# Mixer gate of a two-layer recurrent/attention kernel: from units of two channel tiles by two chunks to units of one tile by four

## The reference, cut to what matters

```python
proj = einsum('bld,pd->blp', x, W_in)              # x: 2048 x 256
gate = proj[..., :INTER]                           # INTER = 4096 channels, 8 groups of 512
hbc  = silu(conv(proj[..., INTER:INTER+CONV_DIM])) # x, B, C of the state space part
...
g  = y * silu(gate)                                # y: the state space output
gg = g * rsqrt(mean(g * g, per group) + EPS)       # norm over the 512 channels of a group
return einsum('bli,di->bld', gg * norm_weight, W_out)
```

## Time and profile before

| | |
|---|---|
| three runs | 2546.90, 2548.81, 2554.18 us; median 2548.81 |
| the profiled execution, its own time | 2549.98 us |
| its span, first to last instruction | 2548.0 us |
| PE busy in the span | 2262.3 us (89%) |
| DVE, ACT, POOL busy | 1850.7, 1433.1, 1266.7 us |
| mixer, from its first load to its last product | 219 to 1518 us of the span |
| slots 0 and 126 start at | 255.37 and 1486.49 us |

### The profile page before, as it was taken

How to read it: one execution, slowest core, us unless ns; L and a number is a source line. 1 busy time by engine, 2 the same in 40 slices (tenths; PEclk the granted TensorE clock), 3 DMA queues, 4 the chain that set the end, 5 groups by cost and what they waited for, 6 DMA issues and landing times. The chain is left out here.

```text
span 2548.0 us, 45522 instructions
## 1 busy us (share of the span) xinstructions
PE 2262.3 (89%) x16164; PEld 1795.5 (70%) x16164; DVE 1850.7 (73%) x3268; ACT 1433.1 (56%) x2447; POOL 1266.7 (50%) x1243
## 2 busy tenths in 40 slices
PE   4995999999999999999999962699999996699993
PEld 3785788888888888888888852588888885344332
DVE  5875777877777777777777746677777776777755
ACT  1333887878787778788778841122222224266661
POOL 3451676777767687676876640344545450000000
PEclk9998999999999999999999985799999998799996
DMA  2003112112121121211111120100000002222214
GB/s 89 1 22 110 49 48 81 45 48 86 53 73 53 44 82 52 82 45 65 61 61 45 53 75 17 35 21 28 21 27 28 21 14 83 70 75 77 80 61 136
DMA packets 91518, 141.17 MB, mean 55 GB/s; under 512 B 23328, under 2 KB 60544, under 8 KB 90048
## 3 DMA queue, kind: packets, MB, share of 16 engines
q1 hardware_dynamic: 89280, 133.96, 15.8%
q10 hardware_dynamic: 2048, 4.72, 0.6%
HBM read 118.12 MB, written 20.32 MB: 54 GB/s over the span
## 5 line engine op out<-in xcount | busy, mean ns | idle before, releaser
L1057 DVE SCALAR_TENSOR_TENSOR mix_cv<-mix_pp,mix_cw,mix_cv 128x384 f32<-128x384 f32 (+4 forms) x864 | 490.7, 571 | 215.2 <-ACT mix_cv L979 194.3
L1004 ACT ACTIVATE mix_lm<-mix_pd 128x512 f32<-128x512 f32 x256 | 153.3, 599 | 207.9 <-PE mix_pd L895 205.9
L1196 POOL TENSOR_TENSOR ffn_hl<-ffn_h,ffn_hh 128x512 fp32r<-128x512 f32 x112 | 144.9, 1294 | 249.9 <-ACT ffn_hh L1254 249.9
L839 POOL TENSOR_TENSOR mix_ce<-mix_ce,mix_cv 128x1024 f32<-128x1024 f32 x112 | 266.7, 2381 | 0.0
L75 PE MATMUL mix_pp<-l0in_XH,mix_w_lo 128*128 128x384 f32 (+2 forms) x576 | 242.9, 422 | 22.6 <-DVE mix_w_lo L1045 16.3
L961 PE MATMUL mix_px<-mix_wo,mix_z 128*128 128x256 f32 x1024 | 257.4, 395 | 0.0
L1719 DVE TENSOR_REDUCE att_tops<-att_psc 128x1 f32<-128x512 f32 (+3 forms) x384 | 189.9, 550 | 56.2 <-PE att_psc L1667 32.2
L845 POOL TENSOR_TENSOR mix_zt<-mix_zsq 128x256 f32<-128x256 f32 x128 | 94.2, 736 | 266.4 <-ACT mix_zsq L1012 266.4
L1743 ACT ACTIVATE att_pr<-att_pst 128x1024 f32<-128x1024 f32 (+7 forms) x256 | 156.5, 657 | 104.0 <-PE att_pst L1684 73.6
L1254 ACT ACTIVATE ffn_hh<-ffn_h 128x512 fp32r<-128x512 f32 x112 | 71.1, 635 | 249.0 <-DVE ffn_h L1277 249.0
L961 PEld LDWEIGHTS mix_px<-mix_wo,mix_z 128*128 128x128 f32 x1024 | 187.4, 193 | 20.8
(11 more groups left out here) (331 smaller groups left out, 6881.0 us busy)
## 6 DMA issues: line engine op xcount, KB each, us to landing
mix_ce<-ecs SPq DMA_DIRECT2D x112, 512.0 KB, 3.7
mix_w_raw<-in_w_in SPq DMA_DIRECT2D x8, 1280.0 KB, 5.5
a_part<-att_sums SPq DMA_DIRECT2D x32, 256.0 KB, 5.1
ffn_raw<-in_wgu SPq DMA_DIRECT2D x56, 128.0 KB, 2.2
mix_ll<-cs SPq DMA_DIRECT2D x384, 4.0 KB
mix_wo<-in_w_out SPq DMA_DIRECT2D x8, 512.0 KB, 6.4
ffn_draw<-in_wd SPq DMA_DIRECT2D x28, 128.0 KB, 2.1
q<-qkv_part SPq DMA_DIRECT2D x24, 128.0 KB, 1.9
```

What stands on the lines that cost most here:

```text
L839: pool.tensor_tensor(ce[o][:, :, :], ce[o][:, :, :], cv[:, CT_C, cols_of(c)].unsqueeze(1).to_broadcast([P, GH, Q]), ALU.mult).then_inc(ce_ ...
L1004: act.activation(lm[o][:, 4 * i:4 * i + 4, :].rearrange("p h l -> p (h l)"), pd[:, :], ACT.Exp).then_inc(l_done, 1)
L1057: last = dve.scalar_tensor_tensor(out, of, cw[:, g, ct, 3 - d:4 - d], out, ALU.mult, ALU.add)
```

## The change

A gate unit now holds one channel tile by four chunks (512 columns) instead of two channel tiles by two chunks (256 columns each): six matmuls of 512 columns in place of twelve of 256. Four units serve four chunks, so a unit has to be ready earlier: slot `c` makes unit c+3 (`LEAD = 3`) instead of c+1, and `sg` grows to two buffers of four chunks.

`w_raw` shrinks to the 768 columns per half of the `x`, `B`, `C` channels. The gate's part comes first, into the same buffer, at SP's step `c % 16 == 1` (512 KB); `wo` follows at step 2; the other 768 KB come at step 6, after POOL has split the gate's part (`wg_split`). The pieces are split in another order, in slots 2 to 5 (gate), 7 to 10 (the rest) and 11 (`wo`). For the first group the gate's raw weights pass through the second half of `sg`, and ACT no longer waits for `wo`.

```diff
-        w_raw = s.sb("w_raw", [P, KD, NXBC + GX])
+        w_raw = s.sb("w_raw", [P, KD, NXBC])
...
-        sg = s.sb("sg", [P, 2, NX, 2 * Q])
+        sg = s.sb("sg", [P, 2, NX, 4 * Q])
...
+        SPLIT_AT = (2, 3, 4, 5, 7, 8, 9, 10, 11)
+        LEAD = 3
...
-                load_weights(0)
+                sp.dma_start(w_raw[:, :, :], w_in[0][:, :, 0:NXBC]).then_inc(wx_in, 16)
+                sp.dma_start(sg[:, 1, 0:KD, :], w_in[0][:, :, NXBC:]).then_inc(wg_in, 16)
+                sp.dma_start(wo[:, 0, :, :], w_out[0]).then_inc(wo_in, 16)
...
+                    if c % 16 == 1 and g < G0 - 1:
+                        wait(sp, gate_done, 16 * g)
+                        sp.wait_ge(wx_split, 2 * (g + 1))
+                        sp.dma_start(w_raw[:, :, 0:GX], w_in[g + 1][:, :, NXBC:]).then_inc(wg_in, 16)
                     if c % 16 == 2 and g < G0 - 1:
+                        wait(sp, op_done, 16 * g)
+                        sp.dma_start(wo[:, (g + 1) % 2, :, :], w_out[g + 1]).then_inc(wo_in, 16)
+                    if c % 16 == 6 and g < G0 - 1:
                         wait(sp, proj_done, 36 * g)
-                        wait(sp, gate_done, 16 * g)
-                        wait(sp, op_done, 16 * g)
-                        sp.wait_ge(wx_split, 2 * (g + 1))
-                        sp.wait_ge(wg_split, 2 * (g + 1))
-                        load_weights(g + 1)
+                        sp.wait_ge(wg_split, 2 * (g + 2))
+                        sp.dma_start(w_raw[:, :, :], w_in[g + 1][:, :, 0:NXBC]).then_inc(wx_in, 16)
...
-                    if live and 4 <= c % 16 < 13 and c // 16 < G0 - 1:
-                        split(c // 16 + 1, c % 16 - 4)
+                    if live and c % 16 in SPLIT_AT and c // 16 < G0 - 1:
+                        split(c // 16 + 1, SPLIT_AT.index(c % 16))
...
                     wait(pe, w_done, u)
-                    wait(pe, ss_done, u - 2)
-                    for t in range(2):
-                        chans = slice(NXBC + (u % 2 * 2 + t) * P, NXBC + (u % 2 * 2 + t + 1) * P)
-                        for i in range(KD):
-                            last = matmul3(pe, pgt[:, t * 2 * Q:(t + 1) * 2 * Q], w_hi[:, o, i, chans], w_lo[:, o, i, chans],
-                                           XH[:, i, at], XL[:, i, at], i == 0, i == KD - 1)
+                    wait(pe, ss_done, u - LEAD - 1)
+                    for i in range(KD):
+                        last = matmul3(pe, pgt[:, :], w_hi[:, o, i, chans], w_lo[:, o, i, chans],
+                                       XH[:, i, at], XL[:, i, at], i == 0, i == KD - 1)
...
-                    if 0 <= c + 1 < NC:
-                        gate(c + 1)
+                    if 0 <= c + LEAD < NC:
+                        gate(c + LEAD)
...
-                act.wait_ge(w_in_s, 32)
+                act.wait_ge(wx_in, 16)
+                act.wait_ge(wg_in, 16)
...
-                        wait(act, z_done, u // 2 * 2 - 2)
-                        act.activation(sg[:, u // 2 % 2, u % 2 * 2:u % 2 * 2 + 2, :].rearrange("p k l -> p (k l)"),
-                                       pgt[:, :], ACT.Silu).then_inc(w_done, 1)
+                        wait(act, z_done, u // 4 * 4 - 4)
+                        if u == 4:
+                            act.wait_ge(wg_split, 2)
+                        act.activation(sg[:, u // 4 % 2, u % 4, :], pgt[:, :], ACT.Silu).then_inc(w_done, 1)
...
-                        dve.wait_ge(w_done, p // 2 * 2 + 2)
+                        dve.wait_ge(w_done, p // 4 * 4 + 4)
```

More of the change, by code:

```diff
@@ L691, in mixer @@
         tabs_in, norm_in, const, made, self_v, zeroed = (s.sem(n) for n in ("tabs_in", "norm_in", "const", "made", "self_v", "zeroed"))
-        w_in_s, wx_split, wg_split, wo_split, hi_made, hi_first = (
-            s.sem(n) for n in ("w_in", "wx_split", "wg_split", "wo_split", "hi_made", "hi_first"))
+        wx_in, wg_in, wo_in, wx_split, wg_split, wo_split, hi_made, hi_first = (
+            s.sem(n) for n in ("wx_in", "wg_in", "wo_in", "wx_split", "wg_split", "wo_split", "hi_made", "hi_first"))
         cs_in, ecs_in = ([s.sem(f"{n}{j}") for j in range(2)] for n in ("cs_in", "ecs_in"))
@@ L764, in _ @@
             def _(sp):
-                def load_weights(g):
-                    sp.dma_start(w_raw[:, :, :], w_in[g]).then_inc(w_in_s, 16)
-                    sp.dma_start(wo[:, g % 2, :, :], w_out[g]).then_inc(w_in_s, 16)
-                load_weights(0)
+                sp.dma_start(w_raw[:, :, :], w_in[0][:, :, 0:NXBC]).then_inc(wx_in, 16)
+                sp.dma_start(sg[:, 1, 0:KD, :], w_in[0][:, :, NXBC:]).then_inc(wg_in, 16)
+                sp.dma_start(wo[:, 0, :, :], w_out[0]).then_inc(wo_in, 16)
                 sp.dma_start(cw[:, :, :, :], conv_w).then_inc(tabs_in, 16)
@@ L809, in split @@
                 def split(g, piece):
-                    o = g % 2
+                    o, k = g % 2, piece // 2 % 2
                     if piece < 8:
[L813 to L817, removed]
+                        part, done, loaded = (slice(NXBC, NXBC + GX), wg_split, wg_in) if piece < 4 else (slice(0, NXBC), wx_split, wx_in)
+                        cols = part.stop - part.start
+                        raw, hi, lo = w_raw[:, k, 0:cols], w_hi[:, o, k, part], w_lo[:, o, k, part]
+                        if piece % 4 == 0:
+                            pool.wait_ge(loaded, 16 * g + 16)
                         if piece % 2 == 0:
@@ L823, in split @@
                     else:
+                        pool.wait_ge(wo_in, 16 * g + 16)
                         pool.tensor_tensor(wo[:, o, :, :], wo[:, o, :, :],
@@ L826, in split @@
                                            ALU.mult).then_inc(wo_split, 1)
-                pool.wait_ge(w_in_s, 32)
                 split(0, 8)
@@ L875, in gate @@
                 def gate(u):
-                    o, at = u // 16 % 2, slice(u // CPS % 2 * (T // 2) + u % CPS // 2 * 2 * Q, u // CPS % 2 * (T // 2) + (u % CPS // 2 + 1) * 2 * Q)
+                    o, at, chans = u // 16 % 2, slice(u % 16 // 4 * 4 * Q, (u % 16 // 4 + 1) * 4 * Q), slice(NXBC + u % 4 * P, NXBC + (u % 4 + 1) * P)
                     if u % 16 == 0:
@@ L952, in _ @@
                         pe.wait_ge(zs_done, p + 1)
-                        pe.wait_ge(w_done, min(c + 2, NC))
+                        pe.wait_ge(w_done, min(c + LEAD + 1, NC))
                         pe.matmul(pgt[:, 0:1], zs[:, :], one[:, :], start=True, stop=True).then_inc(n_done, 1)
@@ L984, in squash @@
                     act.activation(conv_tile(k), conv_tile(k), ACT.Silu).then_inc(conv_done, 1)
-                act.wait_ge(w_in_s, 32)
+                act.wait_ge(wx_in, 16)
+                act.wait_ge(wg_in, 16)
                 for part in (slice(0, NXBC), slice(NXBC, NXBC + GX)):
-                    act.activation(w_hi[:, 0, :, part], w_raw[:, :, part], ACT.Copy).then_inc(hi_first, 1)
+                    raw = w_raw[:, :, :] if part.start == 0 else sg[:, 1, 0:KD, :]
+                    act.activation(w_hi[:, 0, :, part], raw, ACT.Copy).then_inc(hi_first, 1)
                 act.wait_ge(const, 48)
@@ L1020, in _ @@
                         act.activation(btok[o][:, :], pmisc[:, 0:N0], ACT.Copy).then_inc(btok_ready, 1)
-                    if 0 <= c + 1 < NC:
-                        u = c + 1
+                    if 0 <= c + LEAD < NC:
+                        u = c + LEAD
                         act.wait_ge(gate_done, u + 1)
-                        wait(act, z_done, u // 2 * 2 - 2)
-                        act.activation(sg[:, u // 2 % 2, u % 2 * 2:u % 2 * 2 + 2, :].rearrange("p k l -> p (k l)"),
-                                       pgt[:, :], ACT.Silu).then_inc(w_done, 1)
+                        wait(act, z_done, u // 4 * 4 - 4)
+                        if u == 4:
+                            act.wait_ge(wg_split, 2)
+                        act.activation(sg[:, u // 4 % 2, u % 4, :], pgt[:, :], ACT.Silu).then_inc(w_done, 1)
                     if c < 0:
@@ L1044, in _ @@
                     dve.wait_ge(hi_first, 1 if part.start == 0 else 2)
-                    dve.tensor_tensor(w_lo[:, 0, :, part], w_raw[:, :, part], w_hi[:, 0, :, part].bitcast(F32),
+                    dve.tensor_tensor(w_lo[:, 0, :, part], w_raw[:, :, :] if part.start == 0 else sg[:, 1, 0:KD, :], w_hi[:, 0, :, part].bitcast(F32),
                                       ALU.subtract).then_inc(done, 2)
@@ L1078, in _ @@
                         dve.tensor_tensor(z[p % 2][:, :, :], py[:, :].rearrange("p (k l) -> p k l", k=NX),
-                                          sg[:, p // 2 % 2, :, p % 2 * Q:(p % 2 + 1) * Q], ALU.mult).then_inc(z_done, 1)
+                                          sg[:, p // 4 % 2, :, p % 4 * Q:(p % 4 + 1) * Q], ALU.mult).then_inc(z_done, 1)
                     if ks:
```

## The result

The changed kernel takes 2558.72 us, the median of six runs (2557.53 to 2561.23); the kernel before took 2548.86 beside it. The ratio is 1.0036, with a 95% interval of 1.0026 to 1.0047. So it is slower by about 0.3%, where 2546.0 was forecast, and it lies above the forecast's range of 2540 to 2556.

A forecast was written before the change was run, and what follows sets the result against it. PE was taken to wait for ACT's chain from the decays to zs, or to be level with it. The terms -1.0 + 1.7 - 0.7 - 1.3 + 1.2 - 2.7 = -2.8 us took 2548.81 to 2546.0 us, range 2540 to 2556.

The forecast's parts named there:

- second load: SP's 768 KB load at step 6 delays the tables queued behind it; PE stalls 0.25 us seven times, +1.7 us.
- The 4.2: Forecast landing time in us of the 768 KB load after its issue: 5.5 - 1.3.
- The lower bound: For the second load's stall: the shortest landing seen, 5.2 us, was said to make it 0.
- the second load holds up the tables: Rival at step 6's load: a stall of 1.7 us per group makes the kernel 0.3% slower; chance 0.10.
- gate unit, 128 times: PE's cheaper gate matmuls save 0.03 us in a quarter of the 128 slots, -1.0 us; bounds 0 and -7.7.
- wait at step 2: With the large load gone from step 2, PE's one wait for the tables there goes, -0.7 us.
- start: ACT's first copy waits for the two parts of w_in, not for wo; -1.3 us, bounds 0 and -1.3.
- warm-up: Two more gate units between fills in slots -3 and -2 cost at most 2.5 us; half taken, +1.2 us.
- tail: Slots 125 and 126: L954 waits for zs, no longer the gate's Silu; 1.36 us each, -2.7 us.
- The bound of 0: For the tail's gain: PE, with less work there, falls to the lower clock and gives it back.
- PE is the bound after all: Rival in the mixer's slots: the gate units' whole 7.7 us counts, -9.5 us in all, 2539.3 us; chance 0.10.
- The ends give nothing: Rival: warm-up costs its full 2.5 us, the tail gives back its gain; +1.2 us, 2550.0 us; chance 0.12.

The follow-up runs named there:

- e6: Changed kernel with 384 KB of step 6's load left ahead of the tables and the rest moved behind ce; 2551.49 us, ratio 1.0005.
- e7: Changed kernel with wo's 512 KB load moved from step 2 to step 6, so 1280 KB stand ahead of the tables; 2575.27 us, ratio 1.0095.
- e5: Changed kernel with the old gate units, one chunk ahead, and the old sg, so the split loads alone; 2555.60 us, ratio 1.0029.
- e4: Kernel before with the new gate units alone (512 columns, LEAD = 3, larger sg), loads as before; 2548.31 us, ratio 0.9992.
- e8: The changed kernel as it is, measured again in a second series against the kernel before; 2556.41 us, ratio 1.0031.
- e9: Changed kernel with one matmul in place of the three of each gate product, low parts left out; 2568.38 us, ratio 1.0072.
- e1: Changed kernel with the 768 KB load and its two waits moved behind the tables and ce of step 6; 2547.78 us, ratio 0.9998.
- e12: Changed kernel with ScalarE issuing one partition of the 768 KB load in slot 5, SP the other 127 at the end of step 6; 2727.61 us.

## Why the prediction was wrong

The step that failed is the size of the second load's stall: "Give the small tables 0.2 us after the load: PE stalls about 0.25 us, seven times, +1.7 us". It measured 1.10 to 1.49 us, seven times, +8.8. In slot 53 the 1.49 come apart like this: the load went out 5.57 us into the slot (5.47 forecast), it took 4.70 us and not 4.2, and the last table came 0.85 us behind it and not 0.2. The 4.2 took 1.3 us off the landing of 1280 KB for 512 KB less. The 1.3 is what 512 KB add behind a load that is already running, and e6 and e7 agree with it (some 2.5 to 3.0 us per 1024 KB). But between loads that go out by themselves the landing fell by less, from 5.5 us for 1280 KB to 4.7 for 768 KB; why, no run shows. The 0.2 had no row at all.

The lower bound was misread as well. The 5.2 us that "makes it 0" does so only when the same 1.3 us are taken off; as it stands it gives 1.24 us in each group, +8.7 us, which is what came. Still the 8.8 lie inside the bounds, 0 to +23 us, and the rival "the second load holds up the tables" named the right cause, though its own condition, 1.7 us in each group, was not reached. Its chance of 0.10 was too small for a term whose two parts no row showed. Put 8.8 in place of 1.7, and the sum is +4.3 us, about 2553. So the load accounts for 7.1 of the 12.7 us between the forecast and the first result; that the time left the range is also the work of the rest, which follows.

The mechanism was told rightly: the load goes out where POOL's split ends, and `rl` and `ll` queue behind it. That they wait there for its transfer was my estimate, with no row; the trace of the changed kernel shows it, with no small packet in the 3.80 us behind the load's issue and the last table 0.85 us behind its landing.

The other terms, forecast and measured:

| term | forecast | measured |
|---|---|---|
| gate unit, 128 times | -1.0 | 0: the slots keep their length within 0.03 us; PE's wait for `zs` grew by some 0.06 us where there was one |
| second load | +1.7 | +8.8 |
| wait at step 2 | -0.7 | -0.5, slot 81 |
| start | -1.3 | -1.2 (e5, load to slot 0) |
| warm-up | +1.2 | +1.3 (e4), +1.8 beside the split load |
| tail | -2.7 | -3.65 in the first profile, -5.9 in e8; -2.6 with both at the full clock |

The tail was forecast by the right mechanism and size; that the first profile shows 0.95 us more is luck of the granted clock, 0.93 and 0.78 in the one and 0.90 and 0.86 in the other. The bound of 0 took it that PE falls to the lower clock where it has less work, with no row. At the tail the changed kernel had 0.90 and 0.86 once and 1.00 the other time, with the same work; e9, with less, had 0.89 in slot 56, which took 1.17 us more.

With the first profile's values, and its -1.2 + 1.8 = +0.6 ahead of slot 0, the mixer sums to 8.8 - 0.5 + 0.6 - 3.65 = +5.3 us, and it measured 1303.98 - 1298.70 = 5.28. That is 1.0 us above the 4.3: the gate, the warm-up, the start and step 2 came out 1.9 us dearer together and the tail 0.95 better. The other 3.7 us of that profile lie in the stages around it, which the change does not touch and which vary by as much. The medians, +9.9 and +7.2 us in the two series, are above the mixer's 5.3 and 5.0. One reason may be that the profiled execution of the kernel before had a long tail, 22.5 us at 0.93 and 0.78, where its other executions may have had 19.2; only one of them was profiled as it is, so this stays open.

"PE is the bound after all" is refuted by e9: with 0.92 us of PE's work gone a slot keeps its length. "The ends give nothing" is refuted as well: they gave 3.0 us in the first profile, and would give 2.0 with both tails at the full clock.

## What to carry to other kernels

When a load is cut in two, look at what stands behind each piece on its queue and how many microseconds that has to spare, counted from the moment at which the new wait ends; here 17 us of lead became 4, and 768 KB took them. Put the large load behind the small ones that are due in the same slot: in e1 moving it by five issues brought slot 5 back to 9.62 us in all seven groups and cost nothing. And time taken off an engine that only keeps level with another chain buys idle time, which in e9 came with a lower clock, 0.85 to 0.97 in ten slots.

## What the runs showed that was not expected

**A load of 127 partitions ran on what looks like one DMA engine.** In e12 the 762 KB of 127 partitions are issued at 860.82, and SP stands in its next issue for 22 us. SP's timeline, and a window of 5 us in between:

```profile
860.82 0.70 SPq L800 DMA_DIRECT2D mix_w_raw<-in_w_in  x1
861.56 21.93 SPq L792 DMA_DIRECT2D mix_rl<-cs  x1
```

```profile
873.30:878.30 5.00, 0.14 (x1) 0.00 (x0) 1.83 (x4) 0.52 (x1) 1.85 (x2) 0.77 0.07 26
```

The DMA share is 0.07, about one engine in 16, at 26 GB/s. The 128 partitions of the same load land in 4.7 us. Why 127 partitions run so and 128 do not, no run shows.

**Less work on TensorE made the kernel slower.** In e9 the mixer from slot 0 to slot 127 took 10.74 us more than in the changed kernel, 9.8 of it in ten slots at a mean granted clock of 0.85 to 0.97; in slot 56 it was 0.50 from 823.00 to 825.00. Ahead of the fall PE waited longer than in the changed kernel, in slot 56 for 2.00 us where it had been 1.07. The tail of the kernel before has such a fall too: PE waits 1.89 us until 1483.74, and from 1485.01 to 1488.42 its granted clock is 0.50. But such a wait alone does not tell that the clock falls: e5 has the same two waits of 1.89 us, and e8 two of 2.00, with the tail at 1.00.
